# Projections of a differential-attention kernel: halves of the normalisation, the copies of the transposes, and two small steps of the scale

## What is computed

```
xn = (x - mean) / sqrt(var + 1e-5)              # over the last axis
q = rope(xn @ Wq) * 8 ** -0.5                   # 32 heads of 8
k = rope(xn @ Wk)                               # 32 heads of 8
v = xn @ Wv                                     # 16 heads of 16
probs = softmax(q k^T);  w = probs[:, 0] - lam * probs[:, 1]
attn = rms_norm(w v) * subln_g * (1 - lambda_init)
x = x + layernorm(attn @ Wo)
x = x + layernorm(ffn(layernorm(x)))            # tokens chosen by 32 experts
```

## Time and profile before

| | us |
|---|---|
| median of 3 runs | 6013.19 |
| lowest and highest run | 6007.52, 6013.4 |
| the profiled execution's own time | 6007.5 |
| its span, first to last instruction | 6005.7 |
| PE busy | 5596.6 (93%) |
| DVE busy | 5494.2 (91%) |
| ACT busy | 4976.1 (83%) |
| POOL busy | 2065.5 (34%) |

### The profile page before, as it was taken

One profiled execution on the slowest core, in us unless ns is written; L12 is line 12 of the kernel. 1 busy time (PEld: TensorE's weight loads), 2 busy tenths in 40 slices (PEclk: granted clock), 3 DMA queues, 4 the chain that ended last, 5 costly groups with the idle time before them and its releaser, 6 DMA issues. The chain is left out here.

```text
span 6005.7 us, 167689 instructions
## 1 busy us (share of the span) xinstructions
PE 5596.6 (93%) x50896; PEld 1965.7 (33%) x50896; DVE 5494.2 (91%) x6072; ACT 4976.1 (83%) x9206; POOL 2065.5 (34%) x3655
## 2 busy tenths in 40 slices
PE   8878999999999999999999999999999999987775
PEld 4541333333333333333333333333333333325423
DVE  7868999999999999999999999999999999957706
ACT  6665999999999999999999999999999999973304
POOL 7981222222222222222222222222222222236406
PEclk9997999999999999999999999999999999998878
DMA  5671222322222223222322232222232222215598
GB/s 178 204 204 50 52 52 52 52 52 52 52 52 52 53 52 52 53 51 51 54 50 52 52 52 51 51 52 51 51 52 52 52 52 52 52 43 194 177 366 270
DMA packets 469606, 495.27 MB, mean 82 GB/s; under 512 B 132051, under 2 KB 330867, under 8 KB 468963
## 3 DMA queue, kind: packets, MB, share of 16 engines
q1 hardware_dynamic: 467939, 485.74, 34.3%
q10 hardware_dynamic: 1024, 0.53, 0.0%
HBM read 360.60 MB, written 123.21 MB: 81 GB/s over the span
## 5 line engine op out<-in xcount | busy, mean ns | idle before, releaser
L741 DVE TENSOR_REDUCE at_largest<-at_ps_m 128x1 f32<-128x1024 f32 x4096 | 4694.1, 1208 | 46.9 <-PE at_ps_m L845 35.2
L707 ACT ACTIVATE at_e<-at_ps_e 128x512 f32<-128x512 f32 x8192 | 4407.7, 598 | 357.7 <-PE at_ps_e L814 157.5
L831 PE MATMUL at_ps_o<-at_e,at_v 128*32 128x256 f32 (+1 forms) x30720 | 2680.4, 421 | 35.2 <-ACT at_e L707 25.3
L845 PE MATMUL at_ps_m<-k_stack,q_stack 48*128 48x512 bf16 x8192 | 2484.8, 384 | 87.9 <-DVE at_largest L741 55.5
L814 PE MATMUL at_ps_e<-q_stack,k_stack 51*128 51x512 bf16 x8192 | 2515.2, 382 | 7.7 <-issue 2.1
L831 PEld LDWEIGHTS at_ps_o<-at_e,at_v 128*32 128x32 f32 x30720 | 844.9, 149 | 1559.5 <-issue 818.4
L814 PEld LDWEIGHTS at_ps_e<-q_stack,k_stack 51*128 51x128 bf16 x8192 | 568.6, 93 | 1665.8 <-ACT at_e L707 1628.2
L626 POOL TENSOR_TENSOR at_negated<-at_zeros,at_largest_t 128x32 f32<-128x32 f32 x256 | 64.7, 253 | 2169.4 <-DVE at_largest_t L748 2169.4
L845 PEld LDWEIGHTS at_ps_m<-k_stack,q_stack 48*128 48x128 bf16 x8192 | 574.7, 93 | 219.5 <-DVE at_largest L741 188.8
L669 POOL TENSOR_TENSOR at_rms<-at_mean_eps,at_minus_half 128x16 f32<-128x16 f32 x128 | 372.6, 2911 | 10.0
L645 POOL TENSOR_TENSOR at_crossed<-at_totals 128x32 f32<-128x32 f32 x128 | 32.2, 252 | 760.9 <-DMA at_totals<-at_sums 760.9
(11 more groups left out here) (132 smaller groups left out, 3003.0 us busy)
## 6 DMA issues: line engine op xcount, KB each, us to landing
k_stack<-k_parts SPq DMA_DIRECT2D x1536, 64.0 KB
q_stack<-q_parts SPq DMA_DIRECT2D x256, 192.0 KB
q_stack<-q_parts SPq DMA_DIRECT2D x256, 128.0 KB
w_first<-in_w SPq DMA_DIRECT2D x32, 1024.0 KB, 11.7
ex_w_second<-in_w SPq DMA_DIRECT2D x32, 1024.0 KB, 12.7
q_parts<-pr_parts SPq DMA_DIRECT2D x96, 256.0 KB, 2.5
k_parts<-pr_parts SPq DMA_DIRECT2D x96, 256.0 KB, 2.8
pr_x_in<-in_x SPq DMA_DIRECT2D x16, 1024.0 KB, 6.0
```

The source lines that it names most:

```text
L707: nc.scalar.activation(e[:, j % E_BUFS], ps_e[:, bank(u, j)], ACT.Exp, scale=SCALE).then_inc(exp_done, 1)
L741: nc.vector.reduce_max(largest[:, u % 2, j // SIDE, j % SIDE:j % SIDE + 1], ps_m[:, j % 2], AX.X).then_inc(max_done, 1)
L831: last = nc.tensor.matmul(ps_o[32 * tile:32 * tile + 32, columns], v[:, u, tile // 2, first:first + 2 * VD * TILES - kt:TILES], e[:, (QUAD ...
L845: last = nc.tensor.matmul(ps_m[:, j % 2, half * HALF:(half + 1) * HALF], q_stack[rows, u, pair, c, t * P:(t + 1) * P], k_stack[rows, u, pa ...
```

## The change

The normalisation of a batch is done in two halves: the first four tiles in ACT's slot 0, the others in slot 1, each with its own increment of `xn_ready` (two for each batch now). PE waits for the first half before bank 0 and for the second before bank 2. ACT copies banks 0 and 1 in slot 2 and banks 2 and 3 in slot 3, and in each of these slots the copies stand behind the first and second part and ahead of v. DVE makes -mean and var + eps behind the aggregates, and POOL's scale is the power and one product.

```diff
-            eps, minus_half, zeros = sb("eps", [P, TILES]), sb("minus_half", [P, TILES]), sb("zeros", [P, TILES])
+            minus_half = sb("minus_half", [P, TILES])
...
-            shift, bias = sb("shift", [P, TILES]), sb("bias", [P, TILES])
+            neg_mean, bias = sb("neg_mean", [P, TILES]), sb("bias", [P, TILES])
...
                 def load(n, u):
-                    sp.wait_ge(xn_ready, n - 1)
+                    sp.wait_ge(xn_ready, 2 * (n - 1))
...
             @block.gpsimd
             def _(pool):
-                nc.gpsimd.memset(eps[:], EPS).then_inc(pool_set, 1)
                 nc.gpsimd.memset(minus_half[:], -0.5).then_inc(pool_set, 1)
-                nc.gpsimd.memset(zeros[:], 0.0).then_inc(pool_set, 1)
...
                 def scale(m):
 
                     pool.wait_ge(var_done, m + 1)
-                    nc.gpsimd.tensor_tensor(var[:], mean_var[:, :, 1], eps[:], ALU.add).then_inc(pool_step, 1)
-                    pool.wait_ge(pool_step, 3 * m + 1)
                     if not (isinstance(m, int) and m == 0):
-                        pool.wait_ge(xn_ready, m)
+                        pool.sem_inc(pool_passed, 1)
+                        pool.wait_ge(xn_ready, 2 * m)
                     nc.gpsimd.tensor_tensor(rstd[:], var[:], minus_half[:], ALU.pow).then_inc(pool_step, 1)
-                    pool.wait_ge(pool_step, 3 * m + 2)
-                    nc.gpsimd.tensor_tensor(shift[:], mean_var[:, :, 0], rstd[:], ALU.mult).then_inc(pool_step, 1)
-                    pool.wait_ge(pool_step, 3 * m + 3)
-                    nc.gpsimd.tensor_tensor(bias[:], zeros[:], shift[:], ALU.subtract).then_inc(rstd_done, 1)
+                    pool.wait_ge(pool_step, m + 1)
+                    nc.gpsimd.tensor_tensor(bias[:], neg_mean[:], rstd[:], ALU.mult).then_inc(rstd_done, 1)
...
-                def normalise(m, u):
+                def normalise(m, u, side):
                     act.wait_ge(rstd_done, m + 1)
                     if not (isinstance(m, int) and m == 0):
-                        act.wait_ge(t_done, TILES // 2 * m)
-                    for t in range(TILES):
+                        act.wait_ge(t_done, KC * (2 * m - 1 + side))
+                    for t in range(side * TILES // 2, (side + 1) * TILES // 2):
...
                 def slot(n, i, u, ch, has, more, more2):
                     c = CHUNKS * n + ch
-                    if ch == 3 and more:
-                        for j in range(4):
-                            copy_transposed(n + 1, 1 - u, j)
                     if has(1):
                         first_part(c - 1, n if ch else n - 1, (ch - 1) % RING)
                     if has(2):
                         second_part(c - 2, (ch - 2) % RING)
+                    if ch >= 2 and more:
+                        for j in range(2 * (ch - 2), 2 * (ch - 1)):
+                            copy_transposed(n + 1, 1 - u, j)
...
-                    if ch == 0 and more:
-                        normalise(n + 1, 1 - u)
+                    if ch < 2 and more:
+                        normalise(n + 1, 1 - u, ch)
...
-                normalise(0, 0)
+                for side in range(2):
+                    normalise(0, 0, side)
...
-                    dve.wait_ge(dve_step, m + 1)
+                    dve.wait_ge(dve_step, 2 * m + 1)
...
                     for t in range(TILES):
                         last = nc.vector.bn_aggr(mean_var[:, t], stats[:, t])
-                    last.then_inc(var_done, 1)
+                    last.then_inc(dve_step, 1)
+                    dve.wait_ge(dve_step, 2 * m + 2)
+                    nc.vector.tensor_scalar(neg_mean[:], mean_var[:, :, 0], -1.0, None, ALU.mult)
+                    nc.vector.tensor_scalar(var[:], mean_var[:, :, 1], EPS, None, ALU.add).then_inc(var_done, 1)
...
                 def transposes(m, banks):
-                    pe.wait_ge(xn_ready, m + 1)
                     for j in banks:
+                        if j % KC == 0:
+                            pe.wait_ge(xn_ready, 2 * m + j // KC + 1)
                         pe.wait_ge(t_copied, 4 * m + j - 1 + 2)
```

More of the change, by code:

```diff
@@ L151, in project @@
             v_stored = [sem("v_stored0"), sem("v_stored1")]
-            dve_step, pool_step, passed = sem("dve_step"), sem("pool_step"), sem("passed")
+            dve_step, pool_step, passed, pool_passed = sem("dve_step"), sem("pool_step"), sem("passed"), sem("pool_passed")
             x = io["x"].rearrange("b (t p) d -> b p t d", p=P)
@@ L240, in _ @@
             def _(pool):
-                nc.gpsimd.memset(eps[:], EPS).then_inc(pool_set, 1)
                 nc.gpsimd.memset(minus_half[:], -0.5).then_inc(pool_set, 1)
-                nc.gpsimd.memset(zeros[:], 0.0).then_inc(pool_set, 1)
                 nc.gpsimd.memset(ones[:], 1.0).then_inc(ones_set, 1)
-                pool.wait_ge(pool_set, 3)
+                pool.wait_ge(pool_set, 1)
                 pool.wait_ge(ones_set, 1)
```

## The result

The changed kernel takes 6113.35 us (median of 4 runs, 6111.08 to 6121.51), beside 6010.35 us for the kernel before on the same chip (4 runs, 6004.75 to 6013.4). The ratio is 1.0178, with a 95% interval of 1.0163 to 1.0192: slower by 1.8%; the two medians lie 103 us apart. Forecast were 6135 us and a range of 6088 to 6159.

What follows compares the result with a forecast made beforehand. POOL was taken to set the batch period, PE close behind. 19.65 + 457.8 + 28.9 + 39.6 + 31.5 + 1 = 578.4 against 456.4, 122 us more: 6129.5 profiled, 6135 predicted, range 6088 to 6159.

Steps and rivals of the forecast that it cites:

- The ring: PE's chunk 0 waits for ACT's late copies, behind POOL's add and DVE's products: 32.7 us a batch against 25.8.
- The gap of PE before chunk 0: PE ends a batch's work at 24.8 and idles until 32.7, waiting for ACT's copies: 7.9 us.
- the 8 to 10 us for which POOL should be idle: Sign in the profile: POOL idle for 8 to 10 us in each batch.
- the clock term: PE restarts at half clock after its idle time: 2.1 us in each of 15 batches, bounds 0 and 3.4.
- the tail: Batch 15, from its start to the end of the last third part: 39.6 us before the clock loss.
- The DMA argument: ACT's waits for stores behind the stack loads, 15.7 us before, nearly vanish: 1 us left, ends 0 and 15.7.
- The scale: POOL's shorter scale gains 0 behind DVE's products, about 0.9 a batch uncovered; DVE's small steps add 0.4.
- rival 3: PE isn't gated and POOL stays the bound: 0.66 a batch gained, 6003 us, -0.17%; chance 7%.
- The halves: Normalising in halves on ACT: nothing gained or lost inside a batch; first matmul at 19.65 instead of 21.05.
- If the period is 32.7, only the clock term is: Test on PE's batch period, forecast 34.8: at 32.7 only the loss from half clock would be wrong.

Runs made afterwards that it cites:

- e2: Kernel before with only ACT's copies moved behind the parts of slots 2 and 3: 6115.72 us, ratio 1.0181.
- e1: Changed kernel with the copies of banks 2 and 3 ahead of first_part in slot 3: 6006.79 us, ratio 0.9999.
- e3: Kernel before with only the two small scale steps moved to DVE: 6004.01 us, ratio 1.0.
- e4: Kernel before with only the normalisation in halves, in slots 0 and 1, copies in their old place: 6016.98 us, ratio 1.002.
- e5: Changed kernel with eight extra matmuls on PE ahead of its wait before chunk 0: 6092.8 us, ratio 1.0146.
- e6: Changed kernel with the two copies between first_part and second_part: 6111.72 us, ratio 1.0177.
- e7: Changed kernel with the scale as before, four steps on POOL and none on DVE: 6119.93 us, ratio 1.0189.
- f1: Changed kernel with PE filled by extra matmuls before chunk 0 and the copies between the two parts: 6079.48 us, ratio 1.0119.
- f2: Changed kernel with DVE's statistics and POOL's scale late in slot 3: 6066.47 us, ratio 1.0096.
- f4: Kernel before with DVE small steps, late statistics and scale, PE signalled per half, copies heading slots 2 and 3: 5985.33 us, ratio 0.9962.

## Why the prediction was right, point by point

**The ring** was right. Its terms in the batch at 220.07, measured against forecast:

| term | forecast | measured |
|---|---|---|
| chunk 0 to chunk 1, with the clock | 5.16 + 2.1 | 6.85 (5.16 + 1.69) |
| chunk 1 to DVE's first product | 3.72 | 3.64 |
| to the products of chunk 3, small steps in it | 14.55 + 0.4 | 14.85 |
| products to the add of chunk 2 | 2.42 | 2.44 |
| the add, behind DVE's rest | 3.3 | 3.28 |
| CAST, CAST, copies, PE | 3.1 | 3.01 |
| sum | 34.8 | 34.07 |

The gap of PE before chunk 0 was forecast at 7.9 and is 7.74. Wrong is the 8 to 10 us for which POOL should be idle: it waits 9.6 us for the products of chunk 1 and is idle for 11.8 of the 34.19 in all (22.41 busy). The forecast's own figures gave more than 10 too, 34.8 less the 23.70 of rows 1. e2 and e1 show the mechanism from both sides: the copies alone make the loss, and two of them moved ahead of a CAST undo it.

**The sizes.** The last third part ends at 562.65 + 2.12 = 564.8 instead of the forecast 578.4, 13.6 less. Of that:

- 9.0: 13 batches (1 to 13) of 34.11 instead of 34.8, and most of it is *the clock term*, 1.69 instead of 2.1. I took the middle of 1.64 and 2.65, and the near end was right: the clock came back 3.3 us into PE's work, and the loss is that of the stretch after 384.56. The longer end came from the kernel's first matmuls, 6.25 us; the windows there show a granted clock of 1.00, so that they were slow by the clock was argued from their length alone.
- 2.4: batch 0 took 30.34, not 32.7. Nothing of an earlier batch stands in the engines' queues there, and no gap precedes it.
- 0.3: the first matmul at 19.34 instead of 19.65.
- 0.5 and 0.5: batch 14 with 30.46 for 31.0 and the tail with 41.2 for 41.7.
- 1.0: no wait for DMA on this path, where I had left 1.

The other 4 us between the forecast for the profiled execution (6129.5 of 6007.5 + 122) and 6111.44 lie behind the attention's start, where no part of the change is, and 0.6 in the gap ahead of it. The DMA argument held: the stores' wait fell to 3.6.

**The edits that I had costed at nothing** were right inside the ring and wrong as prices of their own. The scale I had valued at "about 0.9 a batch" if its cover were gone, and rival 3 at 0.66; e3 shows no gain, as the earlier add runs into DVE's rest. The step that failed is the length of the add: I counted the move of its start and kept 2.34 for its duration, though the same rows had 3.28 for an add behind a rest. The halves I had at nothing "gained or lost"; by themselves they cost 1.2 a batch (e4); I had looked only at PE's waits and not at POOL's. So even with the ring open rival 3 was too good: it had 0.17% less than the kernel before, and e1, which opens the ring, has 0.9999 of it.

**"If the period is 32.7, only the clock term is" wrong** treated ring and clock as two terms that don't touch each other. e5 bears that out for the filled case (32.49 where the clock holds, 32.7 on average). Without the filling the clock term depends on the ring: it was 1.7 in the changed kernel and 2.65 in e6, whose ring is 0.95 shorter, and both run at 34.1. So some of the closeness is luck. Rings from 31.5 to 32.5 us (the rest in the table under e7, plus the 5.16 from chunk 0 to chunk 1 at full clock) all gave a period of 34.1, so the time would hardly have shown an error of a few tenths in the ring; the terms, as tabled at the head of this section, are the test of it. The same sum for e6 was 13 us off. What sets the length of the low stretch stays open: no run moved PE's gap in time and changed nothing else.

The Trainium skill (TensorE: Matmul & The Clock Gate, HAM oscillation — how this bites in real kernels) says that such a wait is paid for in each turn. The trace agrees: chunk 0 took over 5 us at each steady start, and e5 puts the price at 19 us, against the 32 worked out in the prediction.

## What to carry to other kernels

Before a step is moved behind another on an in-order engine, follow what that other step waits for, and go on until you are either back at the step or at work that is already done: a ring that closes is read off the rows of the kernel before, term by term, to within 0.8 us of 34.8 here. Price a start that moves earlier together with what it then overlaps: here POOL's add took 0.9 us longer beside DVE's rest, which ate the gain. When a gap costs PE its clock, test a shortening with the gap filled too, since the clock hid what it was worth here (0 us in e6, 13 to 16 in f1).

## What was unexpected in the hardware

- The low clock doesn't end a fixed time after PE's restart. It lasts 3.3 us from there in the changed kernel and 5.2 in e6 (6.8 and 10.2 us in all), both after a gap of 7.66 us; chunk 0 takes 5.32 in the one and 6.25 in the other.
- The clock can fall after the gap, when PE is busy again. In f2, after a gap of 2.64, it falls 1.3 us into chunk 0. Ahead of the last batch of the changed kernel PE is idle for 4.07 us; the clock is 1.00 until 523.7, 0.2 us after chunk 0 started, and then 0.50 until 527.1:

```profile
523.52 5.40 PE L436 MATMUL pr_ps_q<-pr_xn_t,pr_w 128*128 128x512 f32 x8 [4.07 <-ACT pr_xn_t L311]
...
519.00:523.00 4.00, 0.45 (x3) 0.05 (x1) 0.00 (x0) 2.50 (x4) 4.00 (x3) 1.00 0.83 197
...
524.00:525.00 1.00, 1.00 (x2) 0.33 (x1) 0.00 (x0) 0.57 (x2) 1.00 (x2) 0.50 0.82 154
```

- A DVE step on eight columns takes 0.84 us in f4, where it ends with POOL's third part; the like step behind it takes 0.16:

```profile
219.36 2.13 POOL L266 TENSOR_TENSOR pr_parts<-pr_rest,pr_parts 128x1024 bf16<-128x1024 f32 x1
220.68 0.84 DVE L376 TENSOR_SCALAR pr_neg_mean<-pr_mean_var 128x8 f32<-128x8 f32 x1
221.43 0.16 DVE L377 TENSOR_SCALAR pr_var<-pr_mean_var 128x8 f32<-128x8 f32 x1
```
